# A transformer layer on one core: joins reordered, identity products in TensorE's gaps, splits by chunk, and the last feed-forward blocks tile by tile

## What is computed

```python
x = x + xattn(layernorm(x), ctx, ...)
#   sa: causal self-attention, 16 heads of 32;   x = ln(sa + x) * g1 + be1
#   ca: attention over the 1601 context tokens;  x = ln(x + ca) * g2 + be2
#   ffn = relu(x @ Wf1 + bf1) @ Wf2 + bf2        (512 -> 2048 -> 512);  x = ln(x + ffn) * g3 + be3
x = x + attn(layernorm(x), ...)
#   gated delta rule, 4 heads of 128, with a short convolution, an exponential average, mixing, rms norm, output projection
x = x + experts(layernorm(x), ...)
#   8 experts, the best 2 for each token, capacity 80 tokens; silu(d @ W1) * (d @ W2) @ W3
```

## Time and profile before

| | |
|---|---|
| median of three runs | 1601.24 us (1597.68 to 1602.25) |
| profiled execution | 1599.45 us, span 1598.2 us |
| mean granted TensorE clock | 0.959 |
| PE busy | 1463.8 us (92%) |
| DVE, ACT, POOL busy | 890.7 (56%), 663.2 (41%), 247.8 us (16%) |

### The profile page before, as it was taken

How to read it: one execution, slowest core, us unless ns; L and a number is a source line. 1 busy time by engine, 2 the same in 40 slices (tenths; PEclk the granted TensorE clock), 3 DMA queues, 4 the chain that set the end, 5 groups by cost and what they waited for, 6 DMA issues and landing times.

```text
span 1598.2 us, 29598 instructions
## 1 busy us (share of the span) xinstructions
PE 1463.8 (92%) x12644; PEld 1121.2 (70%) x12644; DVE 890.7 (56%) x1312; ACT 663.2 (41%) x1207; POOL 247.8 (16%) x169
## 2 busy tenths in 40 slices
PE   7699999999999999999988885995986799999998
PEld 3379888887877878788876674882475476666665
DVE  3632433544445445554355535437867488888886
ACT  1424433433333443334444542431421246666664
POOL 1213211111020101201012232402061000000000
PEclk9989999999999999999999997997988789999999
DMA  7013101101010101101011228006000049999992
GB/s 249 2 44 96 57 30 40 44 21 41 27 39 21 44 24 41 41 21 44 21 44 41 82 81 316 16 0 237 0 3 27 1 146 343 346 345 342 343 338 86
DMA packets 86784, 163.22 MB, mean 102 GB/s; under 512 B 4608, under 2 KB 27136, under 8 KB 86144
## 3 DMA queue, kind: packets, MB, share of 16 engines
q1 hardware_dynamic: 86656, 161.34, 29.2%
HBM read 160.28 MB, written 1.05 MB: 101 GB/s over the span
## 4 chain that ended last, share of the span: by engine, by line
PE 86%; DVE 9%; issue 2%; ACT 1%; POOL 1%; DMA 0%; ACTq 0%; DVEq 0%
PE ring L591 18%; PE ring L581 16%; PE ring L1829 8%; PE turnbank L625 6%; PE pv L1853 4%; PE sc L608 3%; PE pv L644 3%; PE sc L1477 3%; PE sc L1065 3%; PE pv L1829 3%; PE pv L1861 2%; PE ring L1074 1%; PE pv L653 1%; DVE nm L813 1%; PE sc L348 1%
## 5 line engine op out<-in xcount | busy, mean ns | idle before, releaser
L549 POOL TENSOR_TENSOR x_l<-raw,x_h 128x1536 fp32r<-128x1536 f32 (+1 forms) x44 | 159.0, 3615 | 739.6 <-ACT x_h L543 739.6
L1678 DVE TENSOR_TENSOR w_lo<-w_raw,w_hi 128x2048 fp32r<-128x2048 f32 x88 | 200.4, 2285 | 25.3 <-ACT w_hi L1919 25.3
L731 ACT ACTIVATE prob<-sc,nm 128x384 f32<-128x384 f32 (+1 forms) x256 | 153.9, 611 | 118.9 <-DVE nm L818 80.1
L581 PE MATMUL ring<-x_h,wk_h 128*128 128x384 f32 (+1 forms) x512 | 186.4, 364 | 5.4 <-POOL x_l L549 5.4
L591 PE MATMUL ring<-wv_h,x_h 128*128 128x512 f32 (+2 forms) x520 | 190.9, 367 | 0.0
L813 DVE TENSOR_REDUCE nm<-sc 128x2 f32<-128x898 f32 (+1 forms) x128 | 128.0, 1020 | 104.5 <-PE sc L608 104.4
L591 PE MATMUL ring<-wv_h,x_l 128*128 128x512 f32 (+2 forms) x520 | 181.0, 348 | 0.0
L591 PE MATMUL ring<-wv_l,x_h 128*128 128x512 f32 (+2 forms) x520 | 180.7, 348 | 0.0
L581 PE MATMUL ring<-x_h,wk_l 128*128 128x384 f32 (+1 forms) x512 | 177.2, 346 | 0.0
L581 PE MATMUL ring<-x_l,wk_h 128*128 128x384 f32 (+1 forms) x512 | 176.6, 345 | 0.0
L1919 ACT CAST w_hi<-w_raw 128x2048 fp32r<-128x2048 f32 x88 | 167.6, 1907 | 18.4 <-PE pv L1853 15.5
(11 more groups left out here) (442 smaller groups left out, 2549.2 us busy)
## 6 DMA issues: line engine op xcount, KB each, us to landing
w_raw<-in_ew SPq DMA_DIRECT2D x96, 1024.0 KB, 5.3
raw<-in_ctxT SPq DMA_DIRECT2D x33, 768.0 KB, 4.4
raw<-in_ctxT SPq DMA_DIRECT2D x11, 900.0 KB, 4.7
wf<-in_wf SPq DMA_DIRECT2D x2, 4096.0 KB, 19.1
xin<-in_x SPq DMA_DIRECT2D x1, 1024.0 KB, 5.6
w_in<-in_wq SPq DMA_DIRECT2D x1, 1024.0 KB, 7.8
w_in<-in_wk SPq DMA_DIRECT2D x1, 1024.0 KB, 9.9
w_in<-in_wv SPq DMA_DIRECT2D x1, 1024.0 KB, 12.1
```

Source lines behind the costliest of these rows:

```text
L549: pool.tensor_tensor(x_l[x % 3][:, :, 0:w], raw[x % 3][:, :, 0:w], x_h[x % 2][:, :, 0:w].bitcast(F32), ALU.subtract)\
L581: m = pe.matmul(ring[k % 2][:, 0:w], wt[:, c, e:e + P], xt[:, c, 0:w], start=c == 0 and n == 0, stop=c == NC - 1 and n == 2)
L731: act.activation(prob[:, i, 0:WIDTHS[r]], sc[:, i, score_columns(r)], ACT.Exp, bias=nm[:, b % 2, r, h:h + 1], accum_out=psum[:, b % 2, r, ...
L1678: return eng.tensor_tensor(w_lo[n % NSLOT][:, :, :], w_raw[n % NSLOT][:, :, :], w_hi[i % 4][:, :, :].bitcast(F32), ALU.subtract)
```

## The change

- **Splits.** GpSimd makes the low part of a load in four instructions, one for each chunk. ACT's high parts no longer come right behind the job that frees them but behind the exponentials of the next round. GpSimd adds the bias `bv2` once to all tiles at the start of the stage.
- **Joins and norm steps.** Factors, scale and add move into later slots and into the round after next; the norm step is cut in statistics and centre. In the last round denominators, factors, and three quarters of scale and add come ahead of the last mix. The last turned sets of probabilities use three banks in turn.
- **Plan.** The last batch's projections are over the whole context, three key blocks in one segment and one in the next: 40 loads, the same jobs.
- **Feed-forward.** The first six blocks of both weights are loaded from round 56 on into free space. The first hidden product waits chunk by chunk. The last four blocks of `down` are ordered by tile, with second pairs of buffers. The order of norms 3 and 4 is interleaved (`STEPS`), `be3` is added to the residual beforehand, and the last scaling is on ACT with a bias from GpSimd.
- **Identity products.** `pe_keep_busy` issues products of the identity with itself whose result nobody reads: 28 at the start, 18 ahead of the feed-forward, 26 ahead of the gates, 38 ahead of the output projection, 11, 13 and 14 around the router.
- **Sums of squares** are cut in 5, 6 and 5 products behind the projections 9, 10 and 11.

```diff
+    STEPS = ((3, 0), (3, 1), (4, 0), (3, 2), (4, 1), (3, 3), (4, 2), (4, 3))
...
+    def pe_keep_busy(pe, out, n):
+
+        for _ in range(n):
+            pe.matmul(out, ident[:, :], ident[:, :], start=True, stop=True)
+
     def pe_self(pe):
         pe.wait_ge(sem("ident_ready"), 1)
+        pe_keep_busy(pe, bank[7][:, 0:P], 28)
...
-    segment(B - 1, (0, 1), 0, ALL, range(8 * B - 16, 8 * B - 8))
-    segment(B - 1, (2,), 1, FAR, range(8 * B - 8, 8 * B - 5))
-    segment(B - 1, (3,), 1, NEAR, range(8 * B - 5, 8 * B - 3))
+    segment(B - 1, (0, 1, 2), 0, ALL, range(8 * B - 16, 8 * B - 8))
+    segment(B - 1, (3,), 1, ALL, range(8 * B - 8, 8 * B - 3))
...
-        pool.tensor_tensor(x_l[x % 3][:, :, 0:w], raw[x % 3][:, :, 0:w], x_h[x % 2][:, :, 0:w].bitcast(F32), ALU.subtract)\
-            .then_inc(sem("ctx_low"), 1)
+        for c in range(NC):
+            pool.tensor_tensor(x_l[x % 3][:, c, 0:w], raw[x % 3][:, c, 0:w], x_h[x % 2][:, c, 0:w].bitcast(F32), ALU.subtract)\
+                .then_inc(sem("ctx_low"), 1)
...
+        pool.tensor_tensor(xa[:, :, :], xa[:, :, :], over_tiles(bv2[:, :]), ALU.add).then_inc(sem("bias_added"), 1)
...
-        pe.wait_ge(sem("ctx_low"), x + 1)
+        pe.wait_ge(sem("ctx_low"), NC * (x + 1))
...
+    def act_splits_behind(act, jobs):
+
+        for k in jobs:
             if k in LAST_JOB and JOBS[k][1] + 2 < NX:
                 act_split(act, JOBS[k][1] + 2)
...
+            if n > 0:
+                for s in range(1, slots_of(n - 1)):
+                    act_splits_behind(act, PLAN[n - 1][s])
+            act_splits_behind(act, PLAN[n][0])
+            if n % 8 == 0 and n > 0:
+                act_join(act, n // 8 - 1)
...
+            if n == NR - 1:
+                dve_denominators(dve, link, n // 2)
+                dve_join_factors(dve, link, b)
+                dve_join_scale(dve, link, b, range(0, 3))
+                link(dve_join_add(dve, link, b, range(0, 3)))
                 dve_mix(dve, link, n // 2)
...
+            if joins and n % 2 == 0:
+                dve_join_factors(dve, link, b - 1)
+            if n in X_B:
+                dve_x_b_stats(dve, link, X_B.index(n))
             dve_jobs(dve, PLAN[n][2])
             if more and n % 2 == 0:
                 dve_turned(dve, n + 1, 2)
+            if n in X_B:
+                dve_x_b_center(dve, link, X_B.index(n))
+            if joins and n % 2 == 0:
+                dve_join_scale(dve, link, b - 1, every)
...
     def sp_ffn(sp):
+        sp.wait_ge(sem("round_scored"), NR - 8)
+        sp.wait_ge(sem("prob_ready"), 4 * (NR - 8))
+        sp.dma_start(wf1[0][:, :, :], w_dram("wf1")[:, :, 0:FIRST_M * P]).then_inc(sem("matrix0_loaded"), 16)
+        sp.dma_start(wf2[0][:, :, :], w_dram("wf2")[:, 0:FIRST_M, :]).then_inc(sem("matrix0_loaded"), 16)
         sp.wait_ge(sem("job_done"), NJ)
...
-    def pe_turn(pe, src, n):
+    def pe_turn(pe, src, n, free, fill):
         for t in range(NT):
+            pe_keep_busy(pe, free, fill[t])
             pe.wait_ge(sem("normed"), NT * n + t + 1)
...
+        link(dve.tensor_tensor(xres[:, :, :], xres[:, :, :], over_tiles(rows3[:, 1, :]), ALU.add))
         for k in range(2, len(SPLITS)):
             split(k)
...
+        for n, t in STEPS:
+            if n == 3:
+                dve.wait_ge(sem("ffn_done"), t + 1)
+                link(dve.tensor_tensor(tmp[:, t, :], bank[4 + t], xa[:, t, :], ALU.add))
+                norm_stats(dve, link, tmp, t)
+                dve.wait_ge(sem("variance_ready"), norm_count(3, t))
+                link(norm_center(dve, tmp, t, rows3[:, 0, :]))
+            else:
+                link(norm_shift(dve, 3, xa, tmp, t, xres[:, t, :]))
                 norm_stats(dve, link, xa, t)
...
+    def act_last_norm(act):
+
+        for t in range(NT):
+            act.wait_ge(sem("shift_scaled"), t + 1)
+            act.activation(tmp[:, t, :], xa[:, t, :], ACT.Identity, scale=rstd[:, t:t + 1], bias=nshift[:, t:t + 1])\
+               .then_inc(sem("normed"), 1)
...
     def pe_ffn(pe):
-        pe_turn(pe, xa, 2)
-        pe.wait_ge(sem("turned_copied"), 12)
+        pe_turn(pe, xa, 2, turnbank[:, 0:P], (0, 0, 0, 14))
+        pe_keep_busy(pe, turnbank[:, 0:P], 4)
...
+        for t, m in ((0, 12), (0, 13), (0, 14), (1, 12), (0, 15), (1, 13), (1, 14), (1, 15)):
+            down_tile(t, m)
+        for t in (2, 3):
+            for m in range(BY_TILE, NH):
+                down_tile(t, m)
...
-        pe_turn(pe, tmp, 3)
+        pe_turn(pe, tmp, 3, bank[3][:, 3 * P:4 * P], (0, 2, 12, 12))
...
-                sum_squares(0)
+            if n >= 9:
+                sum_squares(0, range(0 if n == 9 else 6 * n - 55, 6 * n - 49 if n < 11 else NM))
...
+        pe.wait_ge(sem("o_used"), 1)
+        pe_keep_busy(pe, bank[4][:, 0:P], 38)
...
-        pe_turn(pe, n2, 4)
+        pe_turn(pe, n2, 4, bank[6][:, 0:P], (0, 0, 0, 6))
+        pe_keep_busy(pe, bank[6][:, 0:P], 5)
...
+        pe_keep_busy(pe, bank[6][:, 0:P], 13)
         pe.wait_ge(sem("chosen_ready"), 1)
...
+        pe_keep_busy(pe, bank[6][:, 0:P], 14)
```

More of the change, by code:

```diff
@@ L624, in pe_turn_probs @@
             t0, w = tiles[t]
-            m = pe.transpose(turnbank[0:w, s * P:(s + 1) * P], prob[:, head, t0:t0 + w], ident[:, :])
+            m = pe.transpose(turned_bank(i)[0:w, s * P:(s + 1) * P], prob[:, head, t0:t0 + w], ident[:, :])
         m.then_inc(sem("tiles_turned"), 1)
@@ L889, in dve_cross @@
             more, b = n + 1 < NR, n // 8
-            joins = n % 8 == 0 and n > 0
+            joins, every = n % 8 < 2 and n >= 8, range(0, 4)
             dve_turned(dve, n, last_turn(n))
@@ L1043, in act_ffn @@
                 act.wait_ge(sem("rows_loaded"), 64 + 64)
-                act.wait_ge(sem("matrix1_loaded"), 32)
+            if (what, m) == ("first", FIRST_M):
+                act.wait_ge(sem("matrix1_loaded"), 48)
             if what == "hidden":
@@ L1458, in pe_delta, with sum_squares @@
         k.then_inc(sem("gates_done"), 1)
-        def sum_squares(i):
+        def sum_squares(i, matrices):
             pe.wait_ge(sem("squares_ready"), i + 1)
-            for m in range(NM):
+            for m in matrices:
                 k = pe.matmul(bank[(6, 2)[i]][:, m:m + 1],
                               squares[i][:, m % GH, (m // GH) * P:(m // GH + 1) * P], ones[:, 0:1], start=True, stop=True)
-            k.then_inc(sem("norms_done"), 1)
+            if matrices[-1] == NM - 1:
+                k.then_inc(sem("norms_done"), 1)
         def spread_gamma(h):
```

191 lines of the change are left out of this document (106 added, 85 removed).

## The result

The changed kernel takes 1558.07 us (median of four runs, 1554.54 to 1560.53) beside 1601.74 for the kernel before: a ratio of 0.9731, 95% interval 0.9708 to 0.9754, 43.7 us less. The forecast was 1541 in a range of 1526 to 1568: the time lies in the range, and about a quarter of the expected gain is missing. The profiled execution took 1558.31 us and its span is 1556.8, 41.4 less than the span before, where 58.5 less was predicted.

A forecast was written before the change was run, and what follows sets the result against it. TensorE carried 86% of the chain, so only its idle or lower-clock time could be saved. Terms from start to router summed to −58.5 us against the profiled 1599.45, giving 1541 us, range 1526 to 1568.

The forecast's parts named there:

- Start: Kernel start: fillers before TensorE's first turns let the first projections avoid half clock; −2.8 us, between −0.5 and −3.2.
- Loads 6 and 7: First cross-attention rounds: ACT's deferred splits make GpSimd's parts late for TensorE; +4.3 us, between 0 and +5.5.
- Joins and norm steps: Steady cross-attention rounds: ACT's new order, later steps and four short GpSimd instructions cut waits; −6.6 and −2.8 us.
- Last two batches: End rounds of cross-attention: the new projection plan removes idle time and a slow-clock stretch; −18.2 us, between −9 and −20.
- rival B: Tail rounds bound by scores, maximum, exponential, turn, copy; half of −16.5 left, 1549 us; within the forecast ground's 0.70.
- rival D: Joins and norm steps: four GpSimd instructions in a row keep the port; only −5, 1545 us; within the forecast ground's 0.70.
- End of cross-attention and first down product: Into feed-forward: shorter norm chain, earlier weights, fuller clock, −12 us; an added DVE add delays the down product, +1.3.
- Norms and gates: After feed-forward: tile-by-tile down products let norms 3 and 4 start earlier, gates at full clock; −9.5 us, −7.5 to −11.4.
- Squares: Delta-rule projections: one-column products cut in 5, 6 and 5 hide their loads and keep the clock; −5.2 us.
- Output projection: Delta-rule output projection: 38 fillers in the gap before it raise the clock; −1.5 us, between 0 and −3.
- Router: Around the router: fillers in the gaps bring its products to full clock; −5.5 us, between +1 and −7.9.
- Rival A: Fillers throughout: the clock falls anyway or fillers overshoot; +22.6 us, 1564; chance 0.22, whole or in part.

## Why the prediction was right or wrong

- **Start** (−2.8, −2.2): the size was nearly right, the mechanism half. The runs without identity products are 1.3 and 1.9 us slower at the start than those with them, by the turns. The projections behind the turns last 0.59 us each from the second on in these two, as with identity products, where the second and third lasted 1.06 before. So that part isn't owed to the identity products. Nor does the clock column show the half clock that I named (1.00 from 15 to 18.4 us). What slowed these products before stays open.
- **Loads 6 and 7** (+4.3, +6.2): the mechanism was right and the waits were 2.53 and 2.40 us for 2.6 and 1.7. Left out was what follows a wait: the clock was at half from 170.4 to 173.8, +1.7.

```profile
165.14 3.88 POOL L562 TENSOR_TENSOR x_l<-raw,x_h 128x384 fp32r<-128x384 f32 x4 [19.02 <-ACT x_h L555]
...
169.16 0.41 PE L598 MATMUL ring<-x_h,wk_h 128*128 128x384 f32 x1 [2.53 <-POOL x_l L562]
...
185.53 0.44 PE L598 MATMUL ring<-x_h,wk_h 128*128 128x450 f32 x1 [2.40 <-POOL x_l L562]
```

- **Joins and norm steps** (−9.4, −10.3): the sum was right, the reason was right in part. ACT's order is 5.3 of it, by the run with splits at once. Four instructions alone, in the kernel before, gave 4.9, mostly in the norm rounds; but in the changed kernel one instruction does as well (597.4), since with ACT's splits deferred the subtraction and the centring meet no split. The sign that I had named, both under 1 us, came true for this reason and not by the cutting.
- **Last two batches** (−18.2, −9.5): the step that failed, an overlap that I had put at nothing. I gave each round its idle time from its projections alone, with ACT's old order in mind, and priced the deferral of the splits only against the first use of a load. Its other effect, where GpSimd's work then falls on DVE, I had weighed for the steady rounds but not here. Nor had I asked what waits behind the split in ACT's and GpSimd's own queues: the join's exponential on ACT, the norm's root on GpSimd. The deferral costs 7.3; without it the stage gives −16.7, with 10.5 us idle where I had 7.1. The time comes out near rival B's half, but this is neither rival B nor rival D as I put them, since moving only the splits wins it back: of PE's waits 8.9 us are DVE's late copy, and one of 2.68 hangs on the norm's late root (1.61 with the split at once).
- **End of cross-attention and first down product** (−12 +1.3, −9.7): the first hidden product came 18.1 us behind the scores (28.7 before). My terms ahead of it, 5.6, 2.3 and 2, give 18.8; the "some 17" among the signs had counted the hidden products' own 2.2 as well. These ran at full clock (5.7 us against 7.63). Mis-sized was the wait of the down product: 2.74 us for two adds of 2.29, against +1.3 between 0 and +2. The clock's fall behind it, 1.7 us from 972.5 to 975.9, was not rated at all.
- **Norms and gates** (−9.5, −7.8): right. The term was for the time behind the products, and from their end to that of the gates it is 18.8 us against 28.5, −9.8. The missing 1.9 lies in the down products (83.7 against 81.8), which hold the clock's fall just named. The last norm was ready 11.2 behind the end of the products (11.5 predicted), and the twelve identity products ahead of the last turn then cost 1.9, which my range held.
- **Squares** (−5.2, −2.8): the profiled execution has two stretches of half clock there; traces of other kernels with the same code have one, and the stage at 52.0, −4.5.
- **Output projection** (−1.5, 0): the clock fell at 1197.8, behind the second of four turns, where PE waited 2.15, 1.47, 1.47 and 0.47 us ahead of the turns; I had put products only ahead of the first turn; with some in these gaps too the stage gives −2.8.
- **Router** (−5.5, −5.6): right in sum. The identity products give about 4 in either pair of kernels (28.6 against 24.6, 30.2 against 26.2); the rest is not shown to be theirs.
- **Rival A and the rule behind it**: from the router's first product to the experts the clock was 0.60 before, 0.64 without and 0.86 with identity products, so these raise it. The Trainium skill, "TensorE: Matmul & The Clock Gate", Part 4, speaks of transpose-mode work; whether the turns alone count, no run here separates. Rival A was right in one part: ahead of the feed-forward the identity products cost 0.6 us, and at the gates their overshoot of 1.9 took back what their clock gave.

## What to carry to other kernels

When an engine's work is deferred, look not only at whether it comes in time but at what it will now run beside and what now queues behind it: here the same deferral paid 5 us in long rounds, where the split met nothing urgent, and cost 7 in short ones and 7 at the start. Cutting a GpSimd instruction in four helps a single DVE step that meets it (4.51 to 1.56 us), not a chain of them. Price a wait of PE with the lower clock that may stand behind it (1.7 us here), and put fillers into the gaps up to the next real product, but not so many that they outlast the wait.

## What I had not expected of the hardware

A 64x16 copy on DVE with one input (L876, L877) is held by a GpSimd instruction as long as a two-input subtraction is: 0.93 us under each of four, 3.36 under one. The Trainium skill, "Advanced Engine Details and Errata", VectorE Performance Modes, says that GpSimd instructions and VectorE's two-port ones block each other at the shared port, and gives source and destination in SBUF, as this copy has them, among the conditions of the two-port modes. The runs agree. They add that the next GpSimd instruction doesn't hold a DVE step any longer once the running one has ended: the four steps end at 809.57, 810.54, 811.50 and 812.48, the four GpSimd instructions at 809.54, 810.50, 811.48 and 812.44.

And a wait of PE can cost more than itself. Behind the waits of 1.6 us at 813.8, 2.5 at 169, 2.7 at 859.7 and 2.7 at 972.6 the granted clock was 0.50 for some 3.4 us, where full-clock products would have taken 1.7 us less. But behind those of 2.4 at 185.5 and 898.8 and of 3.1 at 909.3 it stayed at 1.00, and in the kernel with the later adds the wait at the place of the one at 859.7 (2.65 us) had no fall behind it. What decides between the two, these runs don't show.
